# One PSUM accumulator for the four groups of a query block, in an attention and mixture-of-experts kernel

## The reference

```python
y = layernorm(hidden)
y = y + global_latent_attn(rmsnorm(y) * w1)    # causal over all 2048 tokens, 16 heads of 8 values
y = y + local_gqa_attn(rmsnorm(y) * w2)        # causal window of 32 tokens, 16 heads
x = hidden + layernorm(y)
h = layernorm(x)                               # and then a feed-forward part
f = shared_expert(h) + top1_of_8_experts(h)    # ternary weights
out = x + layernorm(f)

def sdpa(q, k, v, mask):                       # 4 query heads share one of the 4 key/value heads
    scores = einsum('bhqd,bhkd->bhqk', q, k) / sqrt(8)
    probs = softmax(where(mask, scores, -1e30))
    return einsum('bhqk,bhkd->bhqd', probs, v)
```

## Time and profile before

| | |
|---|---|
| median of 3 runs | 556.69 us (556.41 to 556.72) |
| the profiled execution | 556.19 us, of which the span of its instructions is 554.5 |
| PE busy | 457.3 us, 82% of the span |
| PEld busy (beside PE) | 248.8 us, 45% |
| DVE busy | 373.9 us, 67% |
| ACT busy | 355.8 us, 64% |
| POOL busy | 194.8 us, 35% |
| mean granted clock of TensorE | 0.947 |

### The profile page before, as it was taken

One profiled execution on the slowest core, in us unless ns is written; L12 is line 12 of the kernel. 1 busy time (PEld: TensorE's weight loads), 2 busy tenths in 40 slices (PEclk: granted clock), 3 DMA queues, 4 the chain that ended last, 5 costly groups with the idle time before them and its releaser, 6 DMA issues.

```text
span 554.5 us, 16532 instructions
## 1 busy us (share of the span) xinstructions
PE 457.3 (82%) x6400; PEld 248.8 (45%) x6400; DVE 373.9 (67%) x1010; ACT 355.8 (64%) x490; POOL 194.8 (35%) x480
## 2 busy tenths in 40 slices
PE   0258778999999989999999999899998997548263
PEld 0124334545464445644654554454545544424241
DVE  2889987675756866788588658667146566765456
ACT  0033857688977979688689878976897986104010
POOL 3555647676601465331056202601043011041101
PEclk9999979899999999999999999999999999858676
DMA  8300000000000000000000000000000000000000
GB/s 203 96 1 1 2 3 1 1 4 3 1 2 3 11 2 4 2 1 13 2 6 8 3 1 12 1 2 11 3 2 2 3 7 6 1 0 12 0 1 9
DMA packets 8811, 6.25 MB, mean 11 GB/s; under 512 B 1816, under 2 KB 8096, under 8 KB 8736
## 3 DMA queue, kind: packets, MB, share of 16 engines
q1 hardware_dynamic: 5312, 2.52, 1.8%
q10 hardware_dynamic: 3424, 2.68, 1.7%
HBM read 4.15 MB, written 1.05 MB: 9 GB/s over the span
## 4 chain that ended last, share of the span: by engine, by line
PE 47%; DVE 31%; POOL 9%; issue 8%; ACT 4%; SPq 1%; DVEq 1%; DMA 1%; POOLq 0%; ACTq 0%
PE osum_g L980 14%; PE scores L953 9%; PE scores L947 4%; PE misc L1088 4%; PE misc L1077 4%; PE misc L980 3%; ACT prob L801 3%; DVE early L1206 2%; PE misc L997 2%; DVE qe_g L1313 2%; DVE early L1478 1%; DVE early L1439 1%; PE misc L907 1%; DVE early L1202 1%; POOL prob L743 1%
## 5 line engine op out<-in xcount | busy, mean ns | idle before, releaser
L801 ACT ACTIVATE prob<-scores 128x1024 f32<-128x1024 f32 (+3 forms) x352 | 308.2, 929 | 100.0 <-PE scores L953 96.9
L980 PE MATMUL osum_g<-prob,V 128*32 128x256 f32 (+1 forms) x2304 | 148.7, 381 | 4.5 <-POOL prob L743 2.9
L953 PE MATMUL scores<-qT,kT 32*128 32x256 f16 (+3 forms) x1520 | 106.6, 257 | 15.6 <-ACT prob L801 11.0
L980 PEld LDWEIGHTS osum_g<-prob,V 128*32 128x32 f32 x2304 | 63.4, 111 | 57.7 <-issue 29.1
L743 POOL TENSOR_SCALAR_AFFINE_SELECT prob<-prob 128x512 f32<-128x512 f32 x64 | 43.2, 690 | 104.7 <-ACT prob L801 104.3
L953 PEld LDWEIGHTS scores<-qT,kT 32*128 32x128 f16 x1520 | 35.8, 92 | 90.5 <-issue 84.0
L760 POOL TENSOR_SCALAR frs<-fmv 128x1 f32<-128x1 f32 x16 | 3.1, 195 | 115.0 <-DVE fmv L1494 114.7
L1088 PE MATMUL misc<-t2T,h1p 128*128 128x512 f16 x128 | 34.6, 419 | 9.1 <-DVE h1p L1471 9.1
L1077 PE MATMUL misc<-early,t1T 128*128 128x256 f16 x256 | 33.6, 291 | 1.4 <-DVEq L1442 1.3
L1478 DVE TENSOR_TENSOR early<-misc,oh 128x512 f32<-128x512 f32 x32 | 22.0, 686 | 15.9 <-PE misc L1088 14.8
L947 PE MATMUL scores<-band,identb 128*32 128x320 bf16 (+1 forms) x512 | 27.4, 305 | 3.0 <-DVEq L1338 2.1
(11 more groups left out here) (228 smaller groups left out, 724.8 us busy)
## 6 DMA issues: line engine op xcount, KB each, us to landing
X<-in_L_attn_hidden_dram SPq DMA_DIRECT2D x8, 128.0 KB, 4.8
early<-in_L_ffn_expert_w_dram ACTq DMA_DIRECT2D x1, 1024.0 KB, 7.9
out_dram<-X SPq DMA_DIRECT2D x16, 64.0 KB, 1.5
rope<-in_rope_dram SPq DMA_DIRECT2D x1, 256.0 KB, 3.7
early<-in_L_ffn_shared_w_dram ACTq DMA_DIRECT2D x2, 128.0 KB, 8.9
band<-in_band_dram ACTq DMA_DIRECT2D x1, 80.0 KB, 3.1
wraw_l<-in_L_attn_l_wq_dram ACTq DMA_DIRECT2D x1, 64.0 KB, 2.7
ident<-in_ident_dram SPq DMA_DIRECT2D x1, 64.0 KB, 2.5
```

The source lines that it names most:

```text
L801: act.activation(prob[:, n % NP, 2 * half:2 * half + 2, lo:hi], src, ACT.Exp, scale=float(HD) ** -0.5 * QSCALE ** -2).then_inc(exp_done, 1)
L953: ins = pe.matmul(scores[:, 512 * m + c:512 * m + c + w], kT[a][rows, g, P * (t % kept[a]):P * (t % kept[a]) + P], qT[a][rows, b % Q_KEPT[ ...
L980: ins = pe.matmul(o[32 * m:32 * m + 32, q:q + w], V[a][:, t % kept[a], g, :], prob[:, n % NP, m, c:c + w], start=(first and k == 0), stop= ...
```

## The change

All four groups of a block are summed in one bank, for G and for L.

- `V` has 160 columns a key tile instead of 128. The four groups' slots stand at columns 0, 48, 96 and 144: 8 of values, 8 of ones, and zeros elsewhere. A product of group g takes the 32 columns from 0, 32, 96 or 128. So groups 0 and 2 have their 16 columns in the first half of the 32, with zeros behind, and groups 1 and 3 in the second half, with zeros ahead.
- Groups 0 and 1 are summed into columns 0 to 255 of the bank, groups 2 and 3 into columns 256 to 511. Each partition range of 32 then holds two groups of one head place. Only the first product of a block starts the sum.
- One copy of 512 columns by ACT replaces four of 256. `o_free` is waited for once a block. L takes one `misc` bank for the four units instead of one each.
- One step `oT` with four transpositions replaces two with four each. DVE's reciprocal is 128x32 and its product 128x256, once a closing.
- The rows of `wo` are put in the matching order ahead of the launch. POOL fills `V` with zeros and then the slots with ones.
- The planner's steps follow. Its constants are new: one summand (`PULL`) for each of 14 classes *and* each of the 8 blocks, in place of a factor and a summand a class; the feed class is cut in two. The assumed times of the other steps stay.

```diff
+VW = 160
+V_AT = [0, 32, 96, 128]
-KNOBS = {
-    "half1": 106.2,
...
+KNOBS = {"half1": 241, "half0": 24, "whole": 0.13, "look": 0}
+PULL = {
...
+    "frontl": (-518.9, -106.4, -149.9, -168.6, -187.2, -62, -341.8, 384.7),
...
+    "feed2": (-482.4, -235.6, -396, 39.9, -84.2, 40.5, 80, 145.4),
 }
...
+        op((ACT_E, "oevac", a, b), 0.58, *[(PE, "pv", a, b, *u) for u in units_of(a, b)], *old(PE, "oT", a, p))
+        op((PE, "oT", a, b), 0.6, (ACT_E, "oevac", a, b), bank=[((DVE, "oT", a, b), 0)])
+        op((DVE, "oT", a, b), 0.8, (PE, "oT", a, b), *old(PE, "onT", a, p))
...
+def kind_of(k):
+
+    if k[0] in ("Q", "E", "M"):
+        return "unit" + "gl"[k[1]], k[2]
+    name = CLASS.get(k[1], "feed1")
+    if name == "weights":
+        return name, 0
+    return (name + "gl"[k[2]], k[3]) if name in ("front", "pv", "oevac", "close") else (name, k[2])
+
+
+def urgency(steps):
     out = {}
     for k, v in levels(steps).items():
...
+        name, b = kind_of(k)
+        out[k] = v + PULL[name][b]
     return out
...
-                pool.memset(V[G][:], 1.0).then_inc(const_ready, 1)
-                pool.memset(V[L][:], 1.0).then_inc(const_ready, 1)
+                pool.memset(V[G][:], 0.0).then_inc(const_ready, 1)
+                pool.memset(V[L][:], 0.0).then_inc(const_ready, 1)
                 pool.wait_ge(const_ready, 4)
+                for a in (G, L):
+                    slots = bass.AP(V[a], HD, [[kept[a] * VW, P], [VW, kept[a]], [48, KVH], [1, HD]])
+                    pool.memset(slots, 1.0).then_inc(const_ready, 1)
...
-                act.copy(oTs[a][:, g, :], o[:, 0:QB]).then_inc(f, 1)
+                act.copy(oTs[a][:].rearrange("p r q -> p (r q)"), o[:]).then_inc(f, 1)
...
-                first, last = [u == x for x in ENDS[(a, b, g)]]
+                first, last = [u == x for x in ENDS[(a, b)]]
...
-                    s = ("pv", L, b, g, 0)
-                    take(pe, s)
+                    s = ("pv", L, b, 0, 0)
+                    if g == 0:
+                        take(pe, s)
...
+                at = QB * (g // 2)
                 for k, (t, q, w, c) in enumerate(ps):
                     for m in range(GRP):
-                        ins = pe.matmul(o[32 * m:32 * m + 32, q:q + w], V[a][:, t % kept[a], g, :],
+                        ins = pe.matmul(o[32 * m:32 * m + 32, at + q:at + q + w], V[a][:, t % kept[a], V_AT[g]:V_AT[g] + 32],
...
-                for g in range(KVH):
-                    ins = pe.transpose(bank(s)[:, P * g:P * g + P], oTs[a][:, g, P * i:P * i + P], ident[:])
+                for i in range(2):
+                    for r in range(2):
+                        ins = pe.transpose(bank(s)[:, P * (2 * i + r):P * (2 * i + r) + P], oTs[a][:, r, P * i:P * i + P], ident[:])
...
+    for name in ("L0_attn_g_wo", "L0_attn_l_wo"):
+        given[name] = np.ascontiguousarray(given[name].reshape(2, 2, GRP, HD, P).transpose(0, 2, 1, 3, 4).reshape(P, P))
```

More of the change, by code:

```diff
@@ L158, in attend @@
                 op(("M", *u), 1.34, ("E", *u))
[L159 to L167, removed]
+            op((PE, "pv", *u), 0.69 if not g else 0.78 if diag else 1.0, ("M", *u) if diag else ("E", *u), (DVE, "proj", a, b),
+               *([(ACT_E, "oevac", G, p)] if g and b else []), *([(PE, "pv", L, b, 0, 0)] if not g and u[2] else []),
+               bank=[((ACT_E, "oevac", L, b), 0)] if not g and not u[2] else ())
     def close(self, a, b):
         op, p = self.op, b - 1
[L171 to L176, removed]
+        old = lambda *k: [k] if b else []
+        op((ACT_E, "oevac", a, b), 0.58, *[(PE, "pv", a, b, *u) for u in units_of(a, b)], *old(PE, "oT", a, p))
+        op((PE, "oT", a, b), 0.6, (ACT_E, "oevac", a, b), bank=[((DVE, "oT", a, b), 0)])
+        op((DVE, "oT", a, b), 0.8, (PE, "oT", a, b), *old(PE, "onT", a, p))
+        op((PE, "onT", a, b), 0.37, (DVE, "oT", a, b), *old(PE, "wo", a, p), bank=[((ACT_E, "onT", a, b), 0)])
         op((ACT_E, "onT", a, b), 0.38, (PE, "onT", a, b))
@@ L251, in levels @@
     return level
-CLASS = {"prep": "weights", "bound": "weights", "ternary": "weights", "wturn": "weights", "scales": "weights",
+CLASS = {"weights": "weights", "prep": "weights", "bound": "weights", "ternary": "weights", "wturn": "weights", "scales": "weights",
          "stat": "front", "norm": "front", "xT": "front", "proj": "front", "ksplit": "front", "split": "front", "kT": "front",
          "qT": "front", "pv": "pv", "oevac": "oevac", "oT": "close", "onT": "close", "wo": "close", "fstat": "norms", "fxa": "norms",
-         "fh": "norms"}
-def urgency(steps, knobs):
+         "fh": "norms", "fw1": "feed2", "fz": "feed2", "fact": "feed2", "fh1": "feed2", "fw2": "feed2", "fw2s": "feed2",
+         "fsel": "feed2", "fsum": "feed2", "fout": "feed2"}
+def kind_of(k):
[6 more added lines that the diff above has]
+def urgency(steps):
     out = {}
     for k, v in levels(steps).items():
[L263 to L267, removed]
+        name, b = kind_of(k)
+        out[k] = v + PULL[name][b]
     return out
@@ L302, in make_plan @@
     ready, ended = dict(steps.earliest), {}
-    waiting, order, free = [[], [], [], []], [[], [], [], []], [0.0] * 4
+    waiting, order, free = [[] for _ in range(4)], [[] for _ in range(4)], [0.0] * 4
     queues = [[("Q", a, b, *u) for b in range(NB) for u in units_of(a, b)] for a in (G, L)]
@@ L331, in bank_wait @@
             t = max(t, at[n - 1])
-        if n and k[1] in ("proj", "qT", "kT", "oT", "xT", "fhT", "pv"):
+        if n and k[1] in GUARDED:
             for x in [x for c, _ in steps.bank[k] for x in need[c] if x != k]:
@@ L416, in number @@
     unit = {u: n for n, u in enumerate(UNIT_LIST)}
-    pv, osum, ends = {}, {}, {}
+    pv, ends = {}, {}
     for s in [s for s in ORDER[PE] if s[0] == "pv"]:
         pv[s[1:]] = len(pv)
-        if s[1] == G and s[2:4] not in osum:
-            osum[s[2:4]] = len(osum)
-        ends.setdefault(s[1:4], [s[1:], s[1:]])[1] = s[1:]
+        ends.setdefault(s[1:3], [s[1:], s[1:]])[1] = s[1:]
     masks = {s[1:]: n for n, s in enumerate([s for s in ORDER[POOL] if s[0] == "qk"])}
-    return unit, pv, osum, masks, ends
-UNIT, PV, OSUM, MASK, ENDS = number()
+    return unit, pv, masks, ends
+UNIT, PV, MASK, ENDS = number()
 def build(nc, x, norm1_w, norm2_w, g_wq, g_kv_down, g_k_up, g_v_up, g_wo, l_wq, l_wk, l_wv, l_wo,
```

79 lines of the change are left out of this document (39 added, 40 removed).

## The result

The changed kernel takes 546.9 us (median of 4 runs, 546.15 to 548.44) against 556.55 before. The ratio is 0.983 with a 95% interval of 0.9808 to 0.9853: 1.7% or 9.5 us faster. The forecast was 543 us, with a range of 532 to 551. The direction and the range hold; 9.5 of the 13.6 us came. The profiled execution took 548.44 us, the slowest of the four, with a span of 546.7.

The account below looks back on a forecast made before the run. PE was taken as the bound from 120 to 460 us, a dependent chain after that. Terms 7.1 + 1.5 + 1.7 + 1.5 + 0 - 1.0 + 3.0 = 13.8 us gave 543 us, range 532 to 551.

Parts of the forecast that it names:

- Transpositions in the PE-bound stage: From 120 to 460 us, half of 22 oT steps go at 0.644 us each: 7.1 us gained, taken in full.
- What is freed is not used: Rival: PE's removed work turns into waits and the order gives nothing; 5.6 us gained, 551 us, chance 0.12.
- the last chain: After 460 us, block 7's two closings and L's first copies between ACT's exponentials get shorter: 1.7 us gained (1.1 to 2.2).
- The start: From 40 to 120 us, fewer transpositions on PE and less DVE work per closing: 1.5 us gained (0 to 2.6).
- ACT, 1.5 us: Cheaper copies on ACT shorten some of PE's 4.0 us of waits for exponentials: 1.5 us gained (0 to 4.0).
- Waits moved: PE's waits for the copy of `osum_g` move from group ends to block ends: 0 taken (-2.8 to +5.6 us).
- the block ends in full: Rival: waits at all seven block ends of `osum_g` show, adding 5.6 us; 548.6 us, chance 0.1.
- The bank of L: One of three `misc` banks is held from L's first product to the last copy: 1.0 us lost (0 to 16).
- The stall in each block that the rival needed: Rival: PE waits for a second free bank, 2.0 us in each of eight blocks; 558 us, chance 0.05 shared with order losing.
- POOL's fills and the products with the values: Larger fills of `V` hide in POOL's idle time, and products keep count and shapes: both cost nothing.
- The new order: All engines' lists replanned with new constants, judged by 7.8 us of delays in the last stage: 3 us gained (-5 to +8).

Follow-up runs that it names:

- new_path_old_order: The changed data path with every engine's instruction list taken over from the kernel before; 557.82 us, ratio 0.9996 to the kernel before.
- eight_copies: The changed kernel with each ACT copy of 512 columns done as eight copies of 64; 549.56 us, ratio 0.984 to the kernel before.
- old_path_searched: The kernel before with its data path kept and its instruction order searched anew through the planner's constants; 548.75 us, ratio 0.9843 to the kernel before.
- new_path_class_order: The changed data path in an order searched anew with a factor and a summand per class; 544.45 us, ratio 0.9757 to the kernel before.
- turns_twice: The changed kernel with the four transpositions of each oT step done twice; 553.18 us, ratio 0.9914 to the kernel before.
- new_path_that_order: The changed data path in the instruction order of old_path_searched; 544.08 us, ratio 0.9767 to the kernel before.

## Why the prediction was right, and where it was not

The time and its direction were right; the account behind them was not. The forecast was 10.8 us from the data path and 3 from the order. The table shows 0 to 4 us from the data path, by the order it stands in, which leaves some 5 to 9 of the changed kernel's 9.5 us for the order. One term was too large and the other too small, and that they add up to a time inside the range is luck.

*Transpositions in the PE-bound stage, 7.1 us "in full".* This is the step that failed. The size was nearly right: a step that goes frees PE for 0.59 us and not 0.644, so 6.5 us. What failed is the premise that "a microsecond of PE work taken away there is worth nearly a microsecond". It holds only if the list gives PE something to do in its place. In the order of before the whole path was worth 1.7 us over the middle, and 1.7 us in the profile of the searched order. In the changed kernel, 6.9 us of such work put back cost 4.7. A busy share of 96% did not mean that PE was the bound: PE's next product of scores stands behind ACT's last read of that half, and in both pairs PE's waits there grew when its work shrank, from 4.2 to 6.5 and from 2.4 to 7.5 us. The page of the kernel before doesn't show PE full throughout either: three slices between the ninth and the thirty-third have an 8, not a 9.

*"What is freed is not used."* I gave this rival 0.12. In the order of before it is what happens, even in full. It was sized at 551 us because I let a third of the PE term, the last chain and 1.5 us elsewhere stand.

*The start.* The forecast was 1.5 us gained. In the order of before it was 4.6 us lost up to block 3 in the profiled execution; 3.4 of them came back in the run in which the clock rose from 0.80 to 0.91 there. I had read the clock of 0.94 in this stage and drawn nothing from it.

*The last chain, 1.7 us.* In new_path_old_order the stage from the last copy of `osum_g` to the end took 556.5 - 469.0 = 87.5 us instead of 88.4: 0.9 gained, near half. The reciprocal cost 0.07 us more than assumed. In the changed kernel L's last closing stood behind expert products anyway: its copy ended at 489.61 and PE turned it at 493.24.

```profile
489.02 0.59 ACT L818 COPY oTs_l<-misc 128x512 f32<-128x512 f32 x1 [3.11 <-PE misc L990]
...
489.75 3.65 PE L1087 MATMUL misc<-early,t1T 128*128 128x256 f16 x32
...
493.24 0.60 PE L1007 MATMUL misc<-ident,oTs_l 128*128 128x128 f32 x4
```

The forecast that this stage would fall to 83 to 86 us was wrong, it rose to 100.2.

*ACT, 1.5 us.* eight_copies shows no such gain, but is too weak to exclude it. The saving in busy time was sized rightly: 16 copies take 9.5 us (4.8 + 4.7) instead of 24. The budget of the Trainium skill, ScalarE: Activation LUTs (Rules for kernel authors), would by an estimate be 0.72 us a copy; the rows show 0.59.

*Waits moved, 0.* The wait for the copy of `osum_g` is gone from the waits, in new_path_old_order too, so the rival of the block ends in full falls: while the 0.59 us copy runs, PE has other products in its list. The prediction had that rival at 5.6 us, which was a slip: 5.6 us is what all seven ends would cost, and the 2.8 us of today would go in exchange, so it should have stood at +2.8 and 545.8 us. The accumulator fills its bank and the kernel guards it as a whole. The Trainium skill, PSUM — Partial Sum Buffer (PSUM bank collisions raise a hardware error), asks for a guard by bank and 32-partition quadrant, or in the simple version by bank; here that guard costs no wait.

*The bank of L, 1.0 lost.* No run isolates it. The longest wait of PE for a bank in the changed kernel is the 3.91 us at 47.5 us, at the start and before any local unit; from 120 us on the longest is 2.2 us, once. The stall in each block that the rival needed doesn't appear.

*POOL's fills and the products with the values, nothing.* The fills took 2.23 + 0.63 + 0.67 us, with 5.96 us idle behind them. The products into `osum_g` take 148.5 us instead of 148.7, so the zeros in `V` cost what the ones had cost.

*The new order, 3 us.* Too small by half or more. The range of -5 to +8 was made from the last stage, where I saw 7.8 us of holes. That stage didn't shrink in the changed kernel, and old_path_searched gains at the start, in the middle and at the end alike. "List order can't make PE's work less" was no bound either, since the order also chooses the splits: 24 more of them are most of the 9.4 us by which the products of scores grew, a cost that the sum didn't have. The order's part was the larger, and old_path_searched shows that it could be had without touching the data path. Which feature of an order brings the gain is not shown: the orders that are as fast as the changed kernel's or faster split 124 to 154 units, and some of them, new_path_class_order's too, leave the local attention of block 6 ahead of the last units of G.

What stays open: how the changed kernel's 9.5 us divide. Its order can't be run on the old path, so the parts are only bracketed, by 4.7 us (turns_twice) and 4.2 us (new_path_that_order) for the path. The 0.7% between new_path_class_order and the other orders of about the same planner's figure is not explained either.

## What to carry to other kernels

When a change to a kernel with a planned order comes with new constants, run the new steps in the old order and search the old steps' order anew: here the second alone gave the whole gain, and the first none. An engine that is 96% busy is a bound only if its idle time does not grow when work is taken from it; where two engines pass a double buffer to and fro, look for that link first. Price an instruction that goes by the distance from its start to the next one's, and one that is added to a row by what the longer row adds. And look in the trace whether an edit did what it was for: one filling here missed its gap, and eight copies added half of the work they were priced at.

## What the runs showed of the hardware

- Four 128x128 float32 transpositions in a row show 0.66 us, eight 1.09 us: 0.107 us for each one added. The next matmul starts 0.59 us after the first of four, 1.02 us after the first of eight.
- A half score unit (the products of two heads, four matmuls) occupies PE for 0.32 us to the next start, a whole one (four heads, eight matmuls) for 0.33, so a split unit of this size costs twice a whole one. Over units of all sizes, 43 made whole took 10.7 us off PE's busy time, 0.25 us each, and the kernel grew slower by 9.4 us.
- The granted clock from 40 to 120 us differs between kernels and doesn't simply follow PE's work: 0.94 in the kernel before, 0.80 with less work in the same order, 0.91 with some put back; but in the changed kernel 0.94, and 0.91 with work added (turns_twice). Each figure is of one profiled execution.
- The DVE reciprocal grows from 252 ns for 16 elements a partition to 342 ns for 32, 5.6 ns an element; the product from 291 ns for 128 to 425 ns for 256, 1.05 ns an element.
- Eight ACT copies of 128x64 in a row from PSUM take 1.04 us of busy time, one copy of 128x512 takes 0.59.
